# Sixteen batches of attention: a loop of two rows per turn, or every row written out

## The reference

```python
xn = _layernorm(x, axis=-1)
x = x + attn(xn) + ffn(xn)

def attn(hidden_states, ...):              # 16 heads of 8
    rk2, rv2 = rel_k[idx], rel_v[idx]      # idx = clip(k - q, -20, 20) + 20
    attn1 = jnp.einsum('bhqd,bhkd->bhqk', q, k)
    attn2 = jnp.einsum('bhqd,qkd->bhqk', q, rk2)
    attn = jax.nn.softmax((attn1 + attn2) / scale, axis=-1)
    w1 = jnp.einsum('bhqk,bhkd->bhqd', attn, v)
    w2 = jnp.einsum('bhqk,qkd->bhqd', attn, rv2)
    return (w1 + w2).transpose(0, 2, 1, 3).reshape(B, S, E) @ Wo.T + bo
```

## Time and profile before

| | |
|---|---|
| median of 3 runs | 2585.8 us (2581.75 to 2586.46) |
| the profiled execution: its own time | 2584.21 us |
| its span, from the first to the last instruction | 2582.4 us |
| PE busy | 2293.3 us (89% of the span) |
| DVE busy | 1905.0 us (74%) |
| ACT busy | 1584.7 us (61%) |
| POOL busy | 1038.4 us (40%) |
| stage `attend` in the profile, rows 0 to 15 on PE | from 282 us to about 1664 us |

### The profile page before, as it was taken

The page is one execution under the profiler, slowest core; times in us unless marked ns, Lnnn a source line. Parts: engine busy times, 40 slices in busy tenths (PEclk is TensorE's granted clock), DMA queues, the critical chain, the costliest instruction groups (busy, mean ns, idle before and its releaser), DMA issues. The chain is left out here.

```text
span 2582.4 us, 102624 instructions
## 1 busy us (share of the span) xinstructions
PE 2293.3 (89%) x37544; PEld 1609.2 (62%) x37544; DVE 1905.0 (74%) x3734; ACT 1584.7 (61%) x3954; POOL 1038.4 (40%) x1350
## 2 busy tenths in 40 slices
PE   5773599999999999999998999869999996999999
PEld 3441477767767677677676777646666664666665
DVE  5663488878878788788787888637676764777777
ACT  3442477778777777777777777637777772232322
POOL 5664445545554555455445554300000002333332
PEclk9886799999999999999999999959999997999999
DMA  6887345544544455455444554300010101101010
GB/s 191 271 271 205 87 108 120 115 108 110 122 107 111 102 124 112 106 116 123 104 115 105 121 112 105 67 25 26 24 37 24 37 25 58 37 24 37 24 37 16
DMA packets 568188, 243.42 MB, mean 94 GB/s; under 512 B 462278, under 2 KB 531526, under 8 KB 563142
## 3 DMA queue, kind: packets, MB, share of 16 engines
q1 hardware_dynamic: 567750, 237.52, 36.7%
HBM read 134.13 MB, written 103.29 MB: 92 GB/s over the span
## 5 line engine op out<-in xcount | busy, mean ns | idle before, releaser
L886 ACT ACTIVATE a_probs<-a_bank_s,a_neg_max 128x512 f32<-128x512 f32 x1024 | 694.6, 684 | 184.2 <-DVE a_neg_max L821 180.1
L821 DVE TENSOR_REDUCE a_neg_max<-a_bank_s 128x2 f32<-128x1024 f32 x512 | 627.0, 1225 | 56.0 <-ACT a_probs L886 3.7
L673 PE MATMUL a_bank_pt<-a_ident,a_probs 128*128 128x128 f32 x4096 | 573.1, 283 | 8.5 <-issue 2.6
L673 PEld LDWEIGHTS a_bank_pt<-a_ident,a_probs 128*128 128x128 f32 x4096 | 445.1, 143 | 116.4 <-issue 79.1
L866 ACT ACTIVATE a_probs_t<-a_bank_pt 128x512 f32<-128x512 f32 x512 | 305.9, 597 | 201.4 <-PE a_bank_pt L673 196.0
L807 DVE COPY a_probs_t<-a_bank_pt 128x512 f32<-128x512 f32 x512 | 350.1, 684 | 32.4 <-PE a_bank_pt L673 24.5
L662 PE MATMUL a_bank_s<-a_k,a_q 48*32 48x512 bf16 (+15 forms) x4096 | 274.1, 290 | 94.0 <-DMA a_kl<-scr_parts 65.0
L699 PE MATMUL a_bank_o<-a_probs_t,a_v 128*32 128x32 f32 (+2 forms) x15872 | 305.8, 228 | 2.0 <-issue 2.0
L699 PEld LDWEIGHTS a_bank_o<-a_probs_t,a_v 128*32 128x32 f32 x15872 | 245.8, 112 | 58.8 <-ACT a_probs_t L866 48.4
L662 PE MATMUL a_bank_s<-a_kl,a_q 48*32 48x204 bf16 (+14 forms) x3840 | 241.4, 266 | 23.6 <-ACT a_probs L886 19.1
L800 DVE TENSOR_TENSOR a_bank_s<-a_bank_s,a_win 128x144 f32<-128x144 f32 (+2 forms) x640 | 164.2, 275 | 125.9 <-PE a_bank_s L662 113.1
(11 more groups left out here) (161 smaller groups left out, 3600.1 us busy)
## 6 DMA issues: line engine op xcount, KB each, us to landing
scr_probs<-a_probs SPq DMA_DIRECT2D x256, 144.0 KB, 5.2
a_raw<-scr_qr SPq DMA_DIRECT2D x256, 96.0 KB
scr_qr<-p_qr SPq DMA_DIRECT2D x64, 320.0 KB, 2.9
a_feat<-scr_probs SPq DMA_DIRECT2D x256, 78.0 KB
scr_parts<-p_sp SPq DMA_DIRECT2D x144, 128.0 KB, 2.9
a_left<-scr_probs SPq DMA_DIRECT2D x256, 64.0 KB, 2.5
a_q<-scr_parts SPq DMA_DIRECT2D x32, 192.0 KB
a_k<-scr_parts SPq DMA_DIRECT2D x32, 192.0 KB
```

The lines of the kernel that those rows point to most:

```text
L673: ins = nc.tensor.transpose(b_pt[bank_of(job)][:, 0, t * P:(t + 1) * P], probs[(u - 1) % 4][:, j, MAX_REL + t * P:MAX_REL + (t + 1) * P], ...
L821: nc.vector.tensor_reduce(neg_max[:, 2 * pair:2 * pair + 2], b_s[:, 2 * pair:2 * pair + 2, :], AX.X, ALU.max, negate=True).then_inc(max_ok, 1)
L886: nc.scalar.activation(probs[u % 4][:, j, MAX_REL:MAX_REL + S], b_s[:, j, :], ACT.Exp, bias=neg_max[:, j:j + 1], accum_out=sums[:, t, j, u ...
```

## The change

The `Fori` loop of `attend` goes. A Python loop calls `row` for each of rows 1 to 15 with plain numbers, so that all 16 rows and the tail stand one behind the other in the program of each engine. Tiles, buffers, waits and the order of the work within a row stay. What goes with the loop are the branch at its end and the register instructions. The program grows: PE has 7,434 instructions before (a matmul with its weight load counted once) and 25,078 after.

```diff
@@ -515,10 +515,8 @@
         def rows(engine, row):
 
             row(0, 0, 0, first=True)
-            with engine.Fori(0, B // 2 - 1) as i:
-                row(i * 2 + 1, 1, i)
-                row(i * 2 + 2, 0, i + 1)
-            row(B - 1, 1, B // 2 - 1)
+            for b in range(1, B):
+                row(b, b % 2, b // 2)
             row(B, 0, B // 2, tail=True)
```

## The result

| | before | after |
|---|---|---|
| median of the runs made side by side | 2584.41 us (2581.75 to 2586.46, 4 runs) | 2542.85 us (2539.15 to 2547.91, 4 runs) |
| ratio | | 0.984, 95% interval 0.982 to 0.986 |
| the profiled execution: its own time | 2584.21 us | 2547.91 us |
| its span | 2582.4 us | 2546.1 us |

The kernel is 41.6 us faster. The profiled execution of after is the slowest of its four runs, 5 us above their median; so the two traces differ by 36.3 us.

What follows compares the result with a forecast made beforehand. PE, busy 89% of the span, was taken to set the time. -31.2 + 0 + 6.7 = -24.5 us from the profiled 2584.2 gave 2559.7, plus 1.6 for the median: forecast 2561 us, 8-in-10 range 2550 to 2578.

Steps and rivals of the forecast that it cites:

- The six branches: In attend, six taken loop branches go: 5.28 us each in hole and slow clock, less row 1's excess, -31.2 us.
- Straight code: In attend's 14 written-out rows, PE waits for instruction packets, at half of row 15's 0.95 us loss: +6.7 us.
- The register instructions: In attend's looped rows, removing them gives 0, with at most 0.3 us a row, 4 us in all.
- rival C: Straight code starves PE in every attend row, with holes long enough to slow the clock: 2612 us, chance 0.04.
- The stages behind: Stages before and behind attend are untouched, so their time does not change: 0.
- A: Rival: straight code in attend costs nothing, each row runs like row 14: about 2555 us, chance 0.2.
- B: Rival: without the branch, PE waits for the next row's keys at six row ends in attend: 2578 us, chance 0.1.

Runs made afterwards that it cites:

- r1 with 64: Kernel before with attend's loop as two turns of six rows, rows 13 to 15 constants, all engines, plus 64 idle increments on PE ahead of row 0: 0.987.
- e2: Kernel before with only PE's attend rows written out with constants, the other four engines keeping the loop of two rows: 0.999 of the kernel before.
- e3: Kernel before with attend written out on the other four engines, PE alone keeping the loop of two rows: 0.994 of the kernel before.
- g1: Changed kernel without PE's 32 increments a row ahead of the score matmuls, the wait now on the first weight load: 0.978 of the kernel before.
- g3: Changed kernel with those 32 increments a row moved behind the score matmuls, the wait on the first weight load: 0.977 of the kernel before.

## Why the prediction was wrong

The direction was right, the time lay below the range: 2542.85 us where 2561 was forecast and 2550 was the low end. The two traces differ by 36.3 us where the sum had 24.5. By its steps:

*The six branches, -31.2 us.* That the rows that end in a branch and those behind it return to a clean row holds: no hole of 3.7 us is left in rows 1 to 14, and the clock column is 0.96 in row 1, 0.98 in rows 10 and 14 and 1.00 in the other rows shown. The size was measured against row 14 of before, 84.35 us, and that was no clean row: rows with registers and without a hole take 83.3 to 83.8 (r1 with 64). But "the branches of the other engines fall in the same hole and give nothing of their own" is right only because all go at once: PE's share alone is worth nothing (e2), the others' 15 us (e3).

*Straight code, +6.7 us.* The mechanism was right, place by place (26 waits of 0.5 us on average and 1.4 at most, in some rows six, in others none), and the size was low: 13.5 us on issue in place of 3.3, so +10.2. That is idle time alone; what a hole costs behind it, in clock and in later waits, isn't in it. What I had no idea of is that the old loop could have been at 1.03 as well as at 0.997, with the same code 128 instructions further on.

*The register instructions, 0: this is the step that failed.* With 31.2 for the branches and 10.2 for the holes, rows 1 to 14 should have lost 21.0 us; they lost 31.1. The other 10.1, 0.7 us in each of 14 rows, is near the difference of the clean rows (0.8) and lies in the 0.2 to 0.8 that the runs with registers leave, 3 to 11 us in all, where the bound was 4. It isn't all certain to be the registers'. In the kernel before with 64 increments, where PE has hardly a hole but the branch's, rows 1 and 14 take 83.6 and 83.7 us, and the twelve rows between them 35.7 us more than twelve like these: 6.0 us a branch, where the sum had 5.2. That would leave 5.6 us for the registers. That the term isn't 0 is what the runs bear out; its exact size, and whose registers they are, stay open. The argument was "Row 15 isn't faster for it". It could be read otherwise in rows that I had shown myself: row 15 idles 2.3 us more on issue than row 14 but is only 0.95 us behind the earlier trace rows. In rival C I put the other 1.35 us down to something that "absorbs". By what the runs with registers show, 0.2 to 0.8 us of it was the gain from the missing register instructions, and I had counted the net of the two as the price of one; the rest of the 1.35 no run explains.

*The stages behind, 0.* They took 7.1 us less in this trace (row 0 and the start took 1.9 more). Over the kernels with the changed `attend` this stretch scatters: 993, 995, 996, 1001 us from ACT's first exponential of row 15 on, 996 to 1001 for three with the old loop. It is at most a few microseconds of the change, and the rest is luck of this trace. The remaining 5 us lie between the profiled run and the median of four.

Of the rivals, A (2555) was nearest in time and wrong in its reason, since straight code does cost something. By the Trainium skill (Runtime: NRT & Kernel Launch, "Instruction fetch mechanics") crossing a block is mostly hidden; the measurement decides here: 13.5 us in the changed kernel, some 42 us of holes that aren't the branch's in the kernel before with 192 increments (65.5 on issue over all lines, less six branches of up to 4), and 0 to 1.3 in g1 and g3, where the rule does hold. B did not come: waits for `a_kl` rose from 4.0 to 6.1 us in all. C has the holes but not their number, and the clock column stays at 1.00 in most rows. Of the other signs, rows 2 to 14 were to take 84.0 to 86.5 us; they took 82.3 to 88.3.

The range was too narrow below because a term was bounded at 4 us by a single row; with the branches' 31.2 as it stands, it was worth 10.

## What to carry to other kernels

Where one row holds both a gain and a loss, don't take its net for either: compare idle time with idle time and work with work. Where a stream of TensorE is too long to be held, as here, its time can depend on where the 16 KB packets' edges fall: before believing an edit of 1 to 3% on such a kernel, shift the stream by 64 and by 128 idle instructions and see whether that alone does as much. And look for waits that stand on an instruction of their own in a dense stream: putting them on the weight load that needs them was worth another 17 us here (0.984 to 0.977 or 0.978), some 40% of what the loop gave.

## What the runs showed of the hardware

- 128 instructions that do nothing, in an idle stretch ahead of the stage, change the kernel before by 82 us of 2,600 (1.030 against 0.997); of the 77.5 us between the traces, 42 are PE's waits for its own instructions.
- The long ones of these holes (0.7 to 1.8 us from one start to the next on PE's queue) stand at one and the same place in a packet of 256 instructions. In the changed kernel sixteen of 17 end 1.3 to 1.6 us after a packet has landed.
- A wait on an instruction of its own, ahead of a weight load that can carry it, brings most of them about; as many instructions without that wait don't (13.5 us on issue against 1.3, g3).
- At a taken branch DVE idles 2.5 to 2.9 us even when PE runs on (e2), and PE then waits up to 1.7 us for it.
